# Mamba and attention in one kernel: the sums of z*C in 64x64 tiles, begun by ScalarE with D*hs, projections in quarter blocks, and new places for the extra work

## The chip, the core and the metric

The kernel runs on one core of a Trainium2 chip. The metric is the device time of one execution in microseconds; the median of the runs stands for a kernel. The engines of the core are named as the profile names them: PE is TensorE (PEld its weight loads), DVE is VectorE, ACT is ScalarE, POOL is GpSimd, SP is SyncE, whose queue issues all transfers here.

## The reference

Eight sequences of 1024 rows and 256 columns pass through a Mamba block and a layer norm, and then through a layer of attention and experts and a second layer norm. The change touches the Mamba block alone. Cut to what matters:

```python
hs, res = split(x @ w_in.T)              # 512 channels each
hs = silu(conv4(hs))                     # depthwise, 4 taps, causal
dt, B, C = split(hs @ w_xproj.T)         # 64, 16, 16 columns
delta = softplus(dt @ w_dt.T + b_dt)
# for each channel d and state n, over the rows t:
z[t] = exp(delta[t] * A) * z[t-1] + delta[t] * hs[t] * B[t, n]
y[t] = sum_n z[t, n] * C[t, n] + D * hs[t]
y = (y * silu(res)) @ w_out.T
x = layernorm(x + y)
```

## The kernel before, in words

The Mamba phase works through the eight sequences b one after the other, each in U = 64 **units** k. The 512 channels are M = 4 blocks m of 128, the 16 states NG = 8 groups g of two, and a unit takes one half j of a block (64 channels) with one group: its tile has 128 partitions, 64 channels for the first state and the same 64 for the second, and 1024 columns, the rows of the sequence. So k // 16 is the block, k // 2 % 8 the group, k % 2 the half. For each unit:

- ScalarE writes dA = exp(A * delta) (line 710), up to four units ahead,
- TensorE writes the input term delta*hs*B into PSUM with 32 small matmuls, each on a 64x64 tile of the array (`dbx`, line 404); there are two places for it, so `dbx(k)` waits until scan k-2 has ended,
- VectorE runs the scan along the columns (line 847, called scan k below); it needs `dbx(k)` and dA of the unit,
- GpSimd multiplies z by C (line 346).

Every second unit TensorE also adds a finished group to the sums over the states, three groups late, so that the products of unit k-5 are needed at unit k (`add`, line 423). It is a matmul with a stack of two identities as the weights, 128 rows onto 64 columns: four matmuls of 512 columns, one for each half of the columns and each half j of the block. The sums stand in the two PSUM banks of `pair(Y)`. At the first group of a block `d_times_hs` starts them: two 128x128 matmuls of the diagonal of D with hs (line 411). At the last group VectorE reads them in `gate` (line 828), and the next block may start when `gate` is done (`s_yg`).

Between the units stands the **extra work**: for the sequence at hand the other blocks' delta (`dt_proj`, `softplus`), u = delta*hs (`make_u`), its transposition (`turn_u`, `take_u`) and the branch of res (`res_proj`, `res_silu`), for the sequence before it the output projection, residual and layer norm (`out_proj`, `residual`, `ln_sums`, `ln_out`), and for the next one the projection of hs, the convolution and the projection to dt, B and C (`in_proj`, `take_raw`, `conv`, `hs_silu`, `x_proj`, `take_x_dbl`, `turn_b`, `make_diag`). All of it is written out by hand as `if k == ...` in the `units` function of each engine; that list of numbers is the order. Each engine works strictly in its order, so what stands behind a waiting instruction waits as well. Banks 6 and 7 of PSUM, `pair(XP)`, take the result of every one of these projections in turn: one may begin when ScalarE or VectorE has read the one before.

All matmuls have float32 operands, and the trace shows each as two instructions. After the Mamba phase, from about 1735 us, the attention phase runs; the change leaves it as it is.

## Time and profile before

| | us |
|---|---|
| median of 3 runs | 3646.37 (3645.26 to 3652.3) |
| the profiled execution | 3649.15 |
| its span, first to last instruction | 3647.3 |
| busy TensorE, VectorE, ScalarE, GpSimd | 3445.1, 3138.9, 2503.8, 1740.2 |
| one sequence of the Mamba phase, first scan to the next first scan | 212.7 |

The span holds eight such sequences, about 50 us of preparation ahead of them and the attention phase behind them. Busy time is the time in which at least one instruction of the engine was under way; matmuls are pipelined, so the distance from one start to the next says what they cost, not their own length.

### The profile page before, as it was taken

The page shows a single profiled execution, that of the slowest core. Times are in us where ns is not written, and L with a number is a line of the kernel's source. Part 1 is how long each engine was busy: PE and PEld are TensorE (multiplying, and loading weights), DVE is VectorE, ACT ScalarE, POOL GpSimd, SP SyncE. Part 2 cuts the span into 40 slices and gives each one's busy share as a digit, 9 for nine tenths or more (in the row PEclk, how much of TensorE's full clock was granted, in tenths as well). Part 3 has the DMA queues.
Part 4 walks back from the last instruction along what each step waited for, and adds up shares of the span by engine and source line. Part 5 has one row for each costly group of instructions (what it writes and reads, how often), then busy time and mean ns, then how long its engine had stood idle before and what let it go on. Part 6 is the DMA issues. An engine that isn't in the chain of part 4 may idle for free.

```text
span 3647.3 us, 119651 instructions
## 1 busy us (share of the span) xinstructions
PE 3445.1 (94%) x52062; PEld 1570.1 (43%) x52062; DVE 3138.9 (86%) x3007; ACT 2503.8 (69%) x3816; POOL 1740.2 (48%) x1562
## 2 busy tenths in 40 slices
PE   7999999999999999999599999999999999999997
PEld 4555555555555555465233323333233332332422
DVE  6898888889888888987698897998979979799796
ACT  4665656666565656664379596895967949779598
POOL 5787878878787887877121311213112121131210
PEclk9999999999999999999799999999999999999999
DMA  4444444444454544443620704207043060340700
GB/s 128 134 121 112 142 112 134 133 134 121 109 146 108 153 117 135 124 117 91 129 36 9 109 2 71 47 2 111 8 64 54 2 105 14 46 72 2 105 2 13
DMA packets 145230, 307.74 MB, mean 84 GB/s; under 512 B 24484, under 2 KB 64068, under 8 KB 144452
## 3 DMA queue, kind: packets, MB, share of 16 engines
q1 hardware_dynamic: 144708, 300.10, 35.7%
q8 instruction: 411, 6.73, 0.8%
q14 instruction: 111, 0.91, 0.1%
HBM read 230.68 MB, written 35.13 MB: 73 GB/s over the span
## 4 chain that ended last, share of the span: by engine, by line
PE 18%; ACT 12%; issue 11%; DVE 10%; DMA 0%; SPq 0%; ACTq 0%; DVEq 0%; POOL 0%
ACT probs L1509 12%; PE ps L1296 6%; PE ps L1281 4%; DVE neg_max L1623 3%; PE ps L1331 2%; PE ps L1398 2%; PE ps L1311 1%; PE ps L1343 1%; DVE acc L1775 1%; PE ps L1242 1%; DVE att L1682 1%; DVE acc L1763 1%; DVE acc L1708 1%; DVE x1T L1605 1%; DVE x1T L1603 1%
## 5 line engine op out<-in xcount | busy, mean ns | idle before, releaser
L346 POOL TENSOR_TENSOR z<-z,c_rep 128x1024 f32<-128x1024 f32 x512 | 1368.7, 2684 | 319.5 <-DVE z L847 311.6
L847 DVE TENSOR_TENSOR_SCAN z<-dA,ps 128x1024 f32<-128x1024 f32 x512 | 1158.1, 2278 | 195.5 <-PE ps L404 144.7
L1509 ACT ACTIVATE probs<-ps,e_scale 128x512 f32<-128x512 f32 x2048 | 1241.2, 702 | 116.2 <-PE ps L1281 113.9
L1623 DVE TENSOR_REDUCE neg_max<-ps 128x1 f32<-128x1024 f32 x1024 | 1187.3, 1215 | 44.3 <-PE ps L1242 43.0
L710 ACT ACTIVATE dA<-rep,a_rep 128x1024 f32<-128x1024 f32 x512 | 565.1, 1142 | 243.7 <-DVE z L847 230.8
L404 PEld LDWEIGHTS ps<-diag,u_t 64*64 64x64 f32 x32768 | 531.0, 135 | 387.0 <-issue 386.5
L1281 PE MATMUL ps<-q_st,k_st 50*128 50x512 f16 x2048 | 632.9, 384 | 31.7 <-ACT probs L1509 28.5
L404 PE MATMUL ps<-diag,u_t 64*64 64x64 f32 x32768 | 598.4, 222 | 59.4 <-DVE z L847 43.3
L1296 PE MATMUL ps<-probs,v_h 128*32 128x256 f32 x8192 | 649.4, 391 | 0.6 <-ACT o_sb L1516 0.6
L1242 PE MATMUL ps<-k_st,q_st 48*128 48x512 f16 x2048 | 600.4, 384 | 7.7 <-DVE neg_max L1623 6.8
L423 PE MATMUL ps<-z,eye 128*64 128x512 f32 x2048 | 497.1, 605 | 0.1
L1210 POOL TENSOR_TENSOR x_in<-x_in,sq_e 128x256 f32<-128x256 f32 x256 | 193.1, 754 | 407.0 <-ACT sq_e L1530 393.5
L1398 PE MATMUL ps<-w_e,x1T 128*128 128x512 f16 x1536 | 358.7, 386 | 17.3 <-DVE acc L1775 14.8
L1281 PEld LDWEIGHTS ps<-q_st,k_st 50*128 50x128 f16 x2048 | 161.1, 93 | 468.6 <-ACT probs L1509 196.7
L1193 POOL TENSOR_SCALAR m_rest<-neg_max 128x8 f32<-128x8 f32 x128 | 31.0, 242 | 669.0 <-DVE neg_max L1623 669.0
L1296 PEld LDWEIGHTS ps<-probs,v_h 128*32 128x32 f32 x8192 | 167.6, 108 | 318.4 <-issue 218.0
L1220 POOL COPY v_h<-v_all 128x80 f32<-128x80 f32 (+1 forms) x256 | 60.0, 236 | 437.6 <-PE ps L1296 437.5
L1530 ACT ACTIVATE sq_e<-ps,comb_s 128x256 f32<-128x256 f32 x256 | 106.4, 471 | 224.8 <-PE ps L1398 169.2
L1398 PEld LDWEIGHTS ps<-w_e,x1T 128*128 128x128 f16 x1536 | 145.1, 99 | 211.6 <-DVE acc L1775 28.7
L423 PEld LDWEIGHTS ps<-z,eye 128*64 128x64 f32 x2048 | 124.6, 136 | 218.5 <-issue 176.5
L1242 PEld LDWEIGHTS ps<-k_st,q_st 48*128 48x128 f16 x2048 | 152.2, 93 | 46.7 <-issue 24.3
L360 PE MATMUL ps<-xT,w_res 128*128 128x512 f32 x256 | 127.0, 618 | 0.0
(183 smaller groups left out, 2875.2 us busy)
## 6 DMA issues: line engine op xcount, KB each, us to landing
c_rep<-c_scratch SPq DMA_DIRECT2D x512, 256.0 KB, 3.9
rep<-delta SPq DMA_DIRECT2D x128, 256.0 KB, 5.5
q_st<-qk_halves SPq DMA_DIRECT2D x192, 128.0 KB, 10.0
k_st<-qk_halves SPq DMA_DIRECT2D x192, 128.0 KB, 10.7
qk_halves<-qk_parts SPq DMA_DIRECT2D x32, 512.0 KB, 10.8
x_nat<-in_x SPq DMA_DIRECT2D x9, 1024.0 KB, 7.2
x_rows<-x_nat SPq DMA_DIRECT2D x9, 1024.0 KB, 7.4
xT<-in_xT SPq DMA_DIRECT2D x8, 1024.0 KB, 7.0
```

What stands on the lines that cost most here:

```text
L346: pool.tensor_tensor(z[:, k % ZR, :], z[:, k % ZR, :], c_rep[:, slot, :], ALU.mult).then_inc(s_zc, 1)
L404: mm = pe.matmul(ps[q * QD:(q + 1) * QD, 2 + 2 * (k % 2) + r, i * TB:(i + 1) * TB], u_t[rows, i, m * P + j * QD:m * P + (j + 1) * QD], dia ...
L423: mm = pe.matmul(ps[j * QD:(j + 1) * QD, half, :], eye[:, :], z[:, (grp * QN + j) % ZR, half * HALF:(half + 1) * HALF], start=False, stop= ...
L710: act.activation(dA[:, k % AR, :], rep[:, slot, :], ACT.Exp, scale=a_rep[:, m, j, g:g + 1]).then_inc(s_da, 1)
L847: dve.tensor_tensor_scan(z[:, k % ZR, :], dA[:, k % AR, :], pair(1 + k % 2), 0.0, ALU.mult, ALU.add).then_inc(s_z, 1)
L1210: pool.tensor_tensor(to, to, scaled[:, i % 2, e, :], ALU.add).then_inc(s_pa, 1)
L1242: mm = pe.matmul(ps[:, 2 * (qt % 2) + half, :], head(q_st, half, QR, h, qt * P, P), head(k_st, half, QR, h, half * HALF, HALF), start=True ...
L1281: pe.matmul(ps[:, ring_bank(("probs", h, 2 * kt + half)), :], head(k_st, half, QM, h, kt * P, P), head(q_st, half, QM, h, half * HALF, HAL ...
L1296: mm = pe.matmul(ps[VC * j:VC * (j + 1), 6, 0:n], v_h[:, kt, :], probs[:, kt, j * n:(j + 1) * n], start=(kt == 0), stop=(kt == TT - 1), sk ...
L1398: mm = pe.matmul(ps[:, EBANK[u], :], x1T[:, x, k, t * P:(t + 1) * P], w_e[:, w, k, e2 * 2 * H:(e2 + 1) * 2 * H], start=(i == 0), stop=(i = ...
L1509: act.activation(probs[:, kt, half * HALF:(half + 1) * HALF], ps[:, ring_bank(("probs", h, 2 * kt + half)), :], ACT.Exp, scale=e_scale[:, ...
L1623: dve.tensor_reduce(neg_max[:, h % 2, qt:qt + 1], pair(qt % 2), AX.X, ALU.max, negate=True).then_inc(s_mx, 1)
```

## The change

Four things change, in the Mamba phase alone.

**The sums of z*C** are made of 64x64 tiles. `add_part` replaces `add` in the units: each group is now eight matmuls of 64 rows onto 64 columns, in two parts of four. In part 0 the first 64 rows (the first state) go to bank 0 and the last 64 to bank 1, in part 1 the other way round, so that no two row halves write to one bank at a time. Part 1 waits for the end of part 0 (`s_half`) and stands behind `dbx(k)`; part 0 of the next group waits for the end of part 1 (`s_y`).

**The start of the sums** moves from TensorE to ScalarE. `seed_sums` writes D*hs into the two banks with one activation after `gate`, and TensorE waits for it (`s_seed`) ahead of the first group of a block. Only the very first block of the run keeps its two matmuls. GpSimd builds one diagonal of D in place of four.

**Projections** are issued in quarter blocks: one matmul of 512 columns for one half of the columns and one half of the 256 contracted rows (`in_part`, `res_part`, `hs_part`), half a row block of the output projection (`out_part`), one half of `x_proj` (`x_half`) and of `dt_proj`.

**The places** of nearly all extra work change on TensorE, ScalarE and VectorE. Transfers and GpSimd's order stay.

```diff
-            def d_times_hs(m):
-                for half in range(2):
-                    pe.matmul(ps[:, half, :], d_diag[:, m, :], hs[:, m, half * HALF:(half + 1) * HALF],
-                              start=True, stop=False, skip_group_check=True)
+            def start_sums(b, m):
+                if b == 0 and m == 0:
...
+                else:
+                    pe.wait_ge(s_seed, b * M + m)
...
+            def add_part(b, grp, part):
+
+                m, g = grp // NG, grp % NG
+                if part == 0:
+                    if g == 0:
+                        start_sums(b, m)
+                    pe.wait_ge(s_zc, b * U + (grp * QN + QN + CZ))
+                    if g:
+                        pe.wait_ge(s_y, b * GR + grp + ZR // QN)
+                else:
+                    pe.wait_ge(s_half, b * GR + grp + 1)
+                for q in range(QS):
+                    rows, half = slice(q * QD, (q + 1) * QD), (q + part) % 2
+                    for j in range(QN):
+                        mm = pe.matmul(ps[j * QD:(j + 1) * QD, half, :], eye[rows, :],
+                                       z[rows, (grp * QN + j) % ZR, half * HALF:(half + 1) * HALF],
+                                       start=False, stop=(g == NG - 1), skip_group_check=True)
+                mm.then_inc(s_y if part else s_half, 1)
...
+                    if k % QN == 0 and late >= 0 and not first:
+                        add_part(late // GR, late % GR, 0)
                     dbx(b, k)
+                    if k % QN == 0 and first:
+                        add_part(late // GR, late % GR, 0)
+                    if late >= 0 and k % QN == (1 if first else 0):
+                        add_part(late // GR, late % GR, 1)
...
+            def seed_sums(b, m):
+
+                act.wait_ge(s_yg, b * M + (m + 1))
+                act.activation(pair(Y), hs[:, m, :], ACT.Copy, scale=d_col[:, m:m + 1]).then_inc(s_seed, 1)
...
+                    if k == 38:
                         res_silu(b, 2)
+                    if k == 38:
                         softplus(b, 3)
+                    if k == 38:
+                        seed_sums(b, 2)
```

**TensorE, units 36 to 42 of the first sequence, before.** L404 is `dbx`, L423 `add`, L411 `d_times_hs`, L367 the projection to delta, L360 the projection of the next sequence's hs; x32 is one unit's `dbx`.

```order
L404 MATMUL ps<-diag,u_t 64x64 x32
L367 MATMUL ps<-x_dbl,w_dt 128x512 x2
L404 MATMUL ps<-diag,u_t 64x64 x64
L411 MATMUL ps<-hs,d_diag 128x512 x2
L423 MATMUL ps<-z,eye 64x512 x4
L404 MATMUL ps<-diag,u_t 64x64 x32
L423 MATMUL ps<-z,eye 64x512 x4
L404 MATMUL ps<-diag,u_t 64x64 x32
L360 MATMUL ps<-x_nat,w_io 128x512 x4
L404 MATMUL ps<-diag,u_t 64x64 x32
L423 MATMUL ps<-z,eye 64x512 x4
L404 MATMUL ps<-diag,u_t 64x64 x32
```

The same place after the change. L405 is `dbx`, L447 `add_part` (x4 is one part), L372 the projection to delta, L360 as before.

```order
L405 MATMUL ps<-diag,u_t 64x64 x32
L447 MATMUL ps<-z,eye 64x512 x4
L372 MATMUL ps<-x_dbl,w_dt 128x512 x2
L405 MATMUL ps<-diag,u_t 64x64 x64
L447 MATMUL ps<-z,eye 64x512 x4
L405 MATMUL ps<-diag,u_t 64x64 x32
L447 MATMUL ps<-z,eye 64x512 x4
L360 MATMUL ps<-x_nat,w_io 128x512 x4
L447 MATMUL ps<-z,eye 64x512 x4
L405 MATMUL ps<-diag,u_t 64x64 x32
L447 MATMUL ps<-z,eye 64x512 x4
L405 MATMUL ps<-diag,u_t 64x64 x32
```

The two matmuls of L411 are gone, the sum of each group stands in two pieces around a `dbx`, and the four blocks of L360 stand one `dbx` earlier, at unit 39 in place of 40.

**ScalarE, units 36 to 42 of the first sequence, before.** L642 is `res_silu`, L622 `softplus`, L710 dA, L660 `take_raw`; a table load stands ahead of each change of function.

```order
L642 ACT_TABLE_LOAD
L642 ACTIVATE s_res<-ps 128x1024
L710 ACT_TABLE_LOAD
L710 ACTIVATE dA<-rep,a_rep 128x1024
L622 ACT_TABLE_LOAD
L622 ACTIVATE delta<-ps 128x1024
L710 ACT_TABLE_LOAD
L710 ACTIVATE dA<-rep,a_rep 128x1024 x5
L660 ACTIVATE sp_e<-ps 128x1024
```

The same place after, from unit 38. L757 is `res_silu`, L732 `softplus`, L753 `seed_sums`, L825 dA, L775 and L776 `take_raw`.

```order
L757 ACT_TABLE_LOAD
L757 ACTIVATE s_res<-ps 128x1024
L732 ACT_TABLE_LOAD
L732 ACTIVATE delta<-ps 128x1024
L753 ACTIVATE ps<-hs,d_col 128x1024
L825 ACT_TABLE_LOAD
L825 ACTIVATE dA<-rep,a_rep 128x1024 x3
L775 ACTIVATE sp_e<-ps 128x1024
L776 ACTIVATE hs<-ps,w_conv 128x1024
```

`res_silu`, `softplus` and the new `seed_sums` now stand in one row with no dA between them.

**VectorE, units 42 to 50 of the first sequence, before.** L847 is the scan, L796 a step of the convolution, L828 `gate`.

```order
L796 SCALAR_TENSOR_TENSOR hs<-sp_e,w_conv,hs 128x1023
L847 SCALAR_TENSOR_TENSOR z<-dA,ps 128x1024 x3
L796 SCALAR_TENSOR_TENSOR hs<-sp_e,w_conv,hs 128x1022
L847 SCALAR_TENSOR_TENSOR z<-dA,ps 128x1024
L796 SCALAR_TENSOR_TENSOR hs<-sp_e,w_conv,hs 128x1021
L847 SCALAR_TENSOR_TENSOR z<-dA,ps 128x1024
L796 SCALAR_TENSOR_TENSOR hs<-sp_w,w_conv,hs 128x1023
L847 SCALAR_TENSOR_TENSOR z<-dA,ps 128x1024
L796 SCALAR_TENSOR_TENSOR hs<-sp_w,w_conv,hs 128x1022
L847 SCALAR_TENSOR_TENSOR z<-dA,ps 128x1024
L796 SCALAR_TENSOR_TENSOR hs<-sp_w,w_conv,hs 128x1021
L847 SCALAR_TENSOR_TENSOR z<-dA,ps 128x1024
```

The same place after, units 41 to 53. L976 is the scan, L925 the convolution, L957 `gate`.

```order
L925 SCALAR_TENSOR_TENSOR hs<-sp_e,w_conv,hs 128x1023
L976 SCALAR_TENSOR_TENSOR z<-dA,ps 128x1024 x4
L925 SCALAR_TENSOR_TENSOR hs<-sp_e,w_conv,hs 128x1022
L976 SCALAR_TENSOR_TENSOR z<-dA,ps 128x1024 x2
L925 SCALAR_TENSOR_TENSOR hs<-sp_e,w_conv,hs 128x1021
L925 SCALAR_TENSOR_TENSOR hs<-sp_w,w_conv,hs 128x1023
L925 SCALAR_TENSOR_TENSOR hs<-sp_w,w_conv,hs 128x1022
L925 SCALAR_TENSOR_TENSOR hs<-sp_w,w_conv,hs 128x1021
L925 SCALAR_TENSOR_TENSOR hs<-sp_e,w_conv,hs 128x1023
L976 SCALAR_TENSOR_TENSOR z<-dA,ps 128x1024 x4
L957 TENSOR_TENSOR s_res<-s_res,ps 128x1024
L976 SCALAR_TENSOR_TENSOR z<-dA,ps 128x1024 x2
```

Five steps of the convolution, which stood behind one scan each, now stand together behind scan 47.

## Rows read from the trace of the kernel before

**Rows 1.** The page: span and busy time by engine.
```profile
span 3647.3 us, 119651 instructions
...
PE 3445.1 (94%) x52062; PEld 1570.1 (43%) x52062; DVE 3138.9 (86%) x3007; ACT 2503.8 (69%) x3816; POOL 1740.2 (48%) x1562
```

**Rows 2.** Windows: one sequence, cut at the ends of scans 8, 31, 49.
```profile
core 0: us, PE busy (x) PEld busy (x) DVE busy (x) ACT busy (x) POOL busy (x), PEclk, DMA share, GB/s
685.38:709.25 23.87, 20.37 (x558) 12.14 (x556) 22.59 (x12) 11.89 (x12) 21.97 (x9) 1.00 0.33 91
709.25:785.95 76.70, 76.05 (x1632) 45.90 (x1632) 63.84 (x45) 46.53 (x52) 57.04 (x23) 1.00 0.44 119
785.95:842.74 56.79, 54.52 (x1273) 29.77 (x1267) 48.44 (x26) 33.14 (x35) 47.91 (x18) 1.00 0.50 142
842.74:898.07 55.33, 52.29 (x1158) 28.31 (x1151) 48.57 (x27) 38.09 (x36) 46.77 (x16) 1.00 0.48 137
sum 212.69, PE 203.24 PEld 116.12 DVE 183.44 ACT 129.64 POOL 173.69; mean PE 50.81 PEld 29.03 DVE 45.86 ACT 32.41 POOL 43.42
```

**Rows 3.** Groups by line in the same sequence.
```profile
L847 DVE TENSOR_TENSOR_SCAN z<-dA,ps 128x1024 f32<-128x1024 f32 x64 | 144.8, 2278 | 25.6 <-PE ps L404 18.1 <-issue 6.4 <-ACT dA L710 1.0
L404 PE MATMUL ps<-diag,u_t 64*64 64x64 f32 x4096 | 74.7, 221 | 9.4 <-DVE z L847 5.7 <-issue 3.7
...
L423 PE MATMUL ps<-z,eye 128*64 128x512 f32 x254 | 61.7, 605 | 0.0
...
L411 PE MATMUL ps<-hs,d_diag 128*128 128x512 f32 x16 | 7.9, 618 | 0.0
```

**Rows 4.** Timeline of TensorE, units 22 to 35: start, us, instruction.
```profile
755.78 1.98 PE L411 MATMUL ps<-hs,d_diag 128*128 128x512 f32 x4
757.70 1.94 PE L423 MATMUL ps<-z,eye 128*64 128x512 f32 x8
...
785.49 2.10 PE L404 MATMUL ps<-diag,u_t 64*64 64x64 f32 x128
787.52 1.94 PE L423 MATMUL ps<-z,eye 128*64 128x512 f32 x8
789.39 1.16 PE L404 MATMUL ps<-diag,u_t 64*64 64x64 f32 x64
790.48 1.98 PE L360 MATMUL ps<-xT,w_res 128*128 128x512 f32 x4
792.39 1.16 PE L404 MATMUL ps<-diag,u_t 64*64 64x64 f32 x64
```

**Rows 5.** Timeline of TensorE, units 40 and 41.
```profile
811.12 3.70 PE L360 MATMUL ps<-x_nat,w_io 128*128 128x512 f32 x8
814.75 1.16 PE L404 MATMUL ps<-diag,u_t 64*64 64x64 f32 x64
```

**Rows 6.** Timeline of VectorE: scans, and what it waits for.
```profile
727.87 0.69 DVE L814 TENSOR_TENSOR x_nat<-x_nat,ps 128x512 f32<-128x512 f32 x1 [2.06 <-PE ps L435]
...
743.29 2.29 DVE L847 TENSOR_TENSOR_SCAN z<-dA,ps 128x1024 f32<-128x1024 f32 x1
...
786.78 6.64 DVE L847 TENSOR_TENSOR_SCAN z<-dA,ps 128x1024 f32<-128x1024 f32 x3 [0.73 <-PE ps L404]
...
815.98 2.29 DVE L847 TENSOR_TENSOR_SCAN z<-dA,ps 128x1024 f32<-128x1024 f32 x1 [2.08 <-PE ps L404]
...
879.20 2.29 DVE L847 TENSOR_TENSOR_SCAN z<-dA,ps 128x1024 f32<-128x1024 f32 x1 [2.35 <-PE ps L404]
```

**Rows 7.** Timeline of ScalarE: a scaled copy of 128x1024.
```profile
833.72 1.11 ACT L661 ACTIVATE hs<-ps,w_conv 128x1024 f32<-128x1024 f32 x1
```

**Rows 8.** Timeline of ScalarE: a table load and softplus.
```profile
672.51 1.28 ACT L622 ACT_TABLE_LOAD   x1 [2.55 <-issue]
673.80 1.02 ACT L622 ACTIVATE delta<-ps 128x1024 f32<-128x1024 f32 x1
```

More of the change, by code:

```diff
@@ L446, in last_out, with x_half @@
                     mm.then_inc(s_o, 1)
+            def x_half(c, n, m, half):
+                mm = pe.matmul(ps[0:XD, 6 + half, :], w_xp[:, m, :], hs[:, m, half * HALF:(half + 1) * HALF],
+                               start=(n == 0), stop=(n == M - 1))
+                if n == M - 1 and half == 1:
+                    mm.then_inc(s_xp, 1)
             def x_proj(c, n, m):
@@ L479, in units @@
                     late = (b * U + k) // QN - 3
[L480 to L481 removed]
+                    first = late >= 0 and late % NG == 0
+                    if k % QN == 0 and late >= 0 and not first:
+                        add_part(late // GR, late % GR, 0)
                     dbx(b, k)
[L483 to L484 removed]
@@ L528, in units @@
+                    if k == 34:
+                        res_part(b, 2, 1, 0)
+                    if k == 35:
+                        res_part(b, 2, 1, 1)
                     if k == 36:
                         pe.wait_ge(s_sr, b * M + 3)
-                        dt_proj(3)
-                    if k == 40 and more:
+                        dt_half(3, 6, 0)
+                    if k == 36:
+                        dt_half(3, 6, 1).then_inc(s_dt, 1)
+                    if k == 39 and more:
                         pe.wait_ge(s_dl, b * M + 4)
@@ new lines, in units @@
+                    if k == 52:
+                        if more:
+                            pe.wait_ge(s_he, RAW * (b * M + 4))
+                        else:
+                            pe.wait_ge(s_ut, b * M + 4)
+                        res_part(b, 3, 0, 0)
+                    if k == 52:
+                        res_part(b, 3, 0, 1)
+                    if k == 52:
+                        res_part(b, 3, 1, 0)
+                    if k == 54:
+                        res_part(b, 3, 1, 1)
@@ new lines, in units @@
+                    if k == 59 and more:
+                        pe.wait_ge(s_hs, c * M + 3)
+                        x_half(c, 2, 2, 0)
+                    if k == 59 and more:
+                        x_half(c, 2, 2, 1)
+                    if k == 59 and more:
+                        pe.wait_ge(s_hs, c * M + 4)
+                        x_half(c, 3, 3, 0)
+                    if k == 59 and more:
+                        x_half(c, 3, 3, 1)
+                    if k == 59 and more:
+                        pe.wait_ge(s_xd, c + 1)
+                        turn_b(7)
@@ L564, in units @@
+                    if k == 59 and more:
+                        dt_half(0, 6, 0)
+                    if k == 59 and more:
+                        pe.wait_ge(s_bc, c + 1)
+                        dt_half(0, 6, 1).then_inc(s_dt, 1)
+                    if k == 60 and more:
+                        turn_u(c, 0, XP)
                     if k == 56 and not more:
```

326 lines of the change are left out of this document (193 added, 133 removed).

## The prediction

> **What bounds the kernel now.** I read the page first: TensorE is busy for 94% of the span and VectorE for 86% [rows 1]. Both are means over two phases, and the change touches the Mamba phase alone, so the second view is the windows of one sequence in the middle of it, 212.69 us long [rows 2]. There TensorE is busy 203.24 us and idle 9.45, VectorE busy 183.44 and idle 29.25; ScalarE with 129.64 and GpSimd with 173.69 have more room. The granted clock is 1.00 in every window, the upper of TensorE's two levels (2.4 GHz). The groups by line say who waits: a scan stood idle for 18.1 of 25.6 us behind `dbx`, while TensorE waited 5.7 us for scans [rows 3]. So TensorE sets the pace in most of a sequence; only in the first of the four windows, the scans 0 to 8, has it 3.5 us of air in 23.87, and VectorE is the fuller one [rows 2].
>
> **Prices on TensorE**, from one start to the next. Two `dbx` in a row take 787.52 - 785.49 = 2.03 us, one ahead of a full matmul 1.09 [rows 4]: 0.94 of its own, and 0.15 for the change of the tile's shape. One `add` takes 789.39 - 787.52 = 1.87 [rows 4]. Eight instructions of full matmuls of 512 columns take 814.75 - 811.12 = 3.63 [rows 5] and four take 792.39 - 790.48 = 1.91 [rows 4], so 0.43 each, 0.86 for one matmul (a **block** below), and 0.19 for the change of shape. `add` has eight instructions of 512 columns: at 0.43 they would take 3.44 one by one, and 1.87 is two side by side (1.72) and 0.15 for the change. `dbx` has 64 instructions of 64 columns, an eighth of 0.43 each, 3.44 one by one: 0.94 is 3.7 side by side. That is the only row with four 64x64 tiles at once.
>
> **The start of the sums.** `d_times_hs` takes 757.70 - 755.78 = 1.92 [rows 4], of which 0.19 are a change of shape; without it 1.73, four times a sequence: 6.9 us less. In its place ScalarE gets an activation that no row shows, one that writes to PSUM. A scaled copy of the same size takes 1.11 [rows 7]; taken as that, it costs 4.4 us of ScalarE's 83 free ones, and nothing by itself. But TensorE waits for it, and dA is queued behind it. Bounds: 1.02 (an activation of this size [rows 8]) and twice 1.11; the difference shows only where TensorE is waiting, at most four times 1.1 us.
>
> **The sums.** A group had eight instructions two abreast, and has sixteen four abreast. At 0.43 a part is 0.86, at the packing of `dbx` 0.94. I take 0.86, since a long matmul has less start to hide. The matmuls' own time stays at 1.72 per group (bounds: 1.72 and 1.88 for four abreast; two abreast is a rival below). What goes are changes of shape: in the two orders I count 124 per sequence before and 57 after, since `add_part` has the shape of `dbx`. 67 times 0.15 to 0.19 is 10 to 12.7; I take 10.7. The waits: part 1 stands behind a `dbx` of 0.94 that covers the end of part 0. Only at the first group of a block do two parts stand together and one waits for the other's end; a matmul lasts 0.6 [rows 3] where the next starts after 0.43, so some 0.3 us, four times a sequence.
>
> TensorE's work per sequence: 203.2 - 6.9 - 10.7 = 185.6, and VectorE's stays at 183.4. Now both have the same load, and the places decide.
>
> **The places.** `dbx(k)` waits for scan k-2, so TensorE can be ahead by one scan, 2.19 us (three in 6.64 [rows 6]), and a larger heap of extra work between two `dbx` makes VectorE wait. I go through the new order by the four windows of [rows 2], with the prices above, 0.3 from the end of a `dbx` that is waited for to its scan, and 0.15 back.
>
> - Scans 0 to 8: TensorE needs 20.2 and VectorE 22.0, with two of its waits at 0.3: 22.6, from 23.9.
> - Scans 9 to 31: the output projection starts one unit earlier, but two blocks' worth of `res_part` more now stand ahead of `dbx(18)`. Summing TensorE's order from `dbx(9)`, it ends at 34.7, so scan 18 starts at 35.0, when it did before (743.29 [rows 6] - 709.25 [rows 2]). `residual(b, 1)` still waits for the fourth row block, as it did for 2.06 us [rows 6], but TensorE sets the pace there anyway. From scan 18 VectorE has 11.1 us to scan 20 and 25.2 to scan 31, and TensorE only 0.9 more: 72.2, from 76.7. Nearly all the gain of this window is in its last third.
> - Scans 32 to 49: here the new order puts more in. Blocks at units 33 to 36 cost VectorE 3 us. At unit 38 ScalarE has `res_silu`, `softplus` and the seed in a row; `softplus` starts when the projection of unit 36 ends and takes 1.28 + 1.02 [rows 8], the seed 1.11 more: TensorE waits 1.6 us for it, with `dbx(39)` behind. Then four blocks at unit 39 keep `dbx(40)` away: 3.5 us (before, 2.08 [rows 6]). Behind scan 47 the fifth convolution step needs `take_raw`, which needs four blocks of unit 49: 3.2. With 49.9 of work and 0.6 of small waits: 60.3, from 56.8. This window gets slower.
> - Scans 50 to 63: VectorE has 45.3; 0.9 for late `dbx`, and the chain from the last convolution over `x_proj`, `take_x_dbl`, `turn_b` to `make_diag` leaves it idle for 3.6 (before 2.35 for one wait of it [rows 6]): 49.8, from 55.3.
>
> The sum is 22.6 + 72.2 + 60.3 + 49.8 = 204.9, and 212.7 - 204.9 = 7.8 us per sequence. Seven sequences give 55; the last has no work for a next one and I put it at 6; the end and the start (three small products fewer on GpSimd, which something else covers) at nothing. 61 of 3649 us in the profiled execution; that one stands 2.8 above the median, so 3646.4 - 61 = 3585, and I say 3584.
>
> **The rivals.**
>
> *TensorE stays the only bound, and its idle time stays at 9.5 us*: 185.6 + 9.5 = 195.1 per sequence, 17.6 less; seven of these and 8 for the last make 131, so 3515. For it: today's order has TensorE that full. Against: VectorE has 183.4 of 195.1 to do, and its heaps (five convolution steps behind one scan) do not lie where TensorE has air. 14%.
>
> *The new places eat the gain*: my third window is worse by 3.5, and another such wait in two windows, 4 us each (the seed behind two table loads at unit 38 is the likeliest place, also for the others), brings 212.7 again: 3646, with 3630 to 3665 around it. For it: everything in the windows is near its limit. Against: TensorE has 17.6 us less to do. 11%.
>
> *Slower: the large tiles overlap less than those of `dbx`.* With two abreast a part costs 1.72, TensorE has 64 * 0.86 = 55 us more, 185.6 + 55 + 9.5 = 250 per sequence, 37 more: 3940. With three abreast a part costs 16 * 0.43 / 3 / 2 = 1.15, TensorE has 18.5 more, 185.6 + 18.5 + 9.5 = 213.6 per sequence: 3653. The gain is gone where a part is over about 1.06, if I take TensorE to set the pace in six tenths of the sequence (7.8 / 0.6 / 64 = 0.2 above 0.86). Against: `dbx` overlaps both row and column halves, with the same kinds of operands. 9%, 4 of it for two abreast. The Trainium skill, "TensorE: Matmul & The Clock Gate", Part 3 (measured speedup against the span model), speaks for it: four row tiles at once gained it a factor of 3.07 and not 4, by which a part would be an estimated 1.12; the 3.7 of `dbx` does not agree.
>
> **How the numbers follow.** The forecast itself has 66%, with 3550 to 3620: an error of 4 us per sequence either way. Two in ten may be left out: the range takes in half of the first rival and the lower part of the second, 3530 to 3632. A difference of 0.2%, 7 us, is about what can be told from none. Faster: 66, 14 and 5 of the second rival's 11 are 85%; same: 4 of the second and 3 of the third, 7%; slower: 8%.
>
> **What would show it.** Step by step in the new profile: `add_part` with four abreast, a part to the next `dbx` in 0.86 to 0.94; TensorE's busy time at 185 to 190 per sequence; the activation into PSUM at 1.0 to 1.2; VectorE idle for about 21 us, of it some 3.5 each ahead of scan 40, the fifth convolution step, and `make_diag`; windows of 22.6, 72.2, 60.3, 49.8. I am wrong if a part is over 1.0, if the third window is not slower than before, or if the sequence is under 200.

## The result, and the profile after

The changed kernel took 3721.5 us (median of four runs), the kernel before 3645.8 beside it: a ratio of 1.020, 95% interval 1.0186 to 1.0215. It is 2% slower, where I had forecast 1.7% faster and a range up to 3632.

The page of the changed kernel, its span, busy times, DMA queues and costliest groups, to be set beside [rows 1] and [rows 3]:

```profile
span 3728.7 us, 123709 instructions
...
PE 3396.3 (91%) x53962; PEld 1566.1 (42%) x53962; DVE 3156.9 (85%) x3007; ACT 2515.2 (67%) x3825; POOL 1676.7 (45%) x1559
...
q8 instruction: 427, 7.00, 0.8%
...
L976 DVE TENSOR_TENSOR_SCAN z<-dA,ps 128x1024 f32<-128x1024 f32 x512 | 1149.3, 2274 | 193.5 <-PE ps L405 134.6
...
L405 PE MATMUL ps<-diag,u_t 64*64 64x64 f32 x32768 | 622.6, 222 | 135.2 <-issue 90.0
```

The same row on the page of the kernel before:

```profile
L404 PE MATMUL ps<-diag,u_t 64*64 64x64 f32 x32768 | 598.4, 222 | 59.4 <-DVE z L847 43.3
```

TensorE is busy for 49 us less than before, and yet the span is 81 longer: both TensorE and VectorE now stand idle more. The last row is the new thing. The matmuls of `dbx` (L405) have 135.2 us of idle time ahead of them, 90.0 of it ended by "issue": nothing that the profile shows was being waited for. Before it was 59.4 us, and 43.3 of that a wait for a scan.

One sequence in the middle, in windows cut at the ends of scans 8, 31 and 49 as in [rows 2]; columns: length, then busy time of each engine, clock, DMA:

```profile
core 0: us, PE busy (x) PEld busy (x) DVE busy (x) ACT busy (x) POOL busy (x), PEclk, DMA share, GB/s
716.94:742.42 25.48, 21.22 (x652) 14.01 (x652) 22.41 (x13) 14.48 (x13) 21.98 (x9) 0.93 0.29 86
742.42:818.42 76.00, 71.64 (x1755) 44.78 (x1753) 63.12 (x45) 45.73 (x49) 56.74 (x23) 1.00 0.46 120
818.42:880.20 61.78, 56.71 (x1274) 31.22 (x1276) 53.73 (x27) 35.65 (x37) 46.15 (x19) 0.97 0.47 130
880.20:935.67 55.47, 48.25 (x1171) 25.89 (x1164) 46.14 (x26) 35.50 (x33) 40.04 (x16) 1.00 0.49 136
sum 218.73, PE 197.82 PEld 115.90 DVE 185.41 ACT 131.38 POOL 164.91; mean PE 49.46 PEld 28.97 DVE 46.35 ACT 32.84 POOL 41.23
```

The forecast was 22.6, 72.2, 60.3 and 49.8. Worked out in the same way for the second to the seventh sequence, the mean windows are 24.1, 78.5, 63.6 and 55.3 us, and 24.6, 77.0, 55.2 and 54.3 in the kernel before. So the third window became longer, as forecast, but by 8.4 us and not by 3.5. Each of the others should have become shorter by 1.3 to 5.5 us, and of them only the first did, by half a microsecond. TensorE is busy for 197.8 us, where 185.6 were forecast.

TensorE in that sequence (start, length, instructions, idle time ahead):

```profile
727.37 1.15 PE L405 MATMUL ps<-diag,u_t 64*64 64x64 f32 x58
731.19 1.29 PE L405 MATMUL ps<-diag,u_t 64*64 64x64 f32 x64 [2.67 <-DVE z L976]
732.19 2.00 PE L447 MATMUL ps<-z,eye 64*64 64x512 f32 x8
...
818.54 0.70 PE L405 MATMUL ps<-diag,u_t 64*64 64x64 f32 x33
820.28 0.69 PE L405 MATMUL ps<-diag,u_t 64*64 64x64 f32 x31 [1.03 <-issue]
...
860.22 1.09 PE L447 MATMUL ps<-z,eye 64*64 64x512 f32 x8
861.13 1.11 PE L405 MATMUL ps<-diag,u_t 64*64 64x64 f32 x64
862.06 1.04 PE L447 MATMUL ps<-z,eye 64*64 64x512 f32 x8
862.92 1.11 PE L405 MATMUL ps<-diag,u_t 64*64 64x64 f32 x64
...
910.47 5.39 PE L473 MATMUL ps<-hs,w_xp 128*96 128x512 f32 x12
916.97 1.11 PE L388 MATMUL ps<-ident,x_dbl 16*64 16x16 f32 x32 [1.11 <-ACT x_dbl L748]
```

Four things are to be seen.

- A part of the sums (L447) takes 0.91 or 0.86 us from its start to the next: the four tiles do work side by side.
- At 818.54 a `dbx` stops after 33 of its 64 instructions and goes on 1.03 us later, with no semaphore waited for.
- After 2.67 us of idle time the granted clock fell to the lower level (1.2 GHz): the part at 732.19 took 2.00 us where others take 1.04 to 1.09. The clock of the first window is 0.93.
- Six half-products of `x_proj` stand in one heap at unit 59 (5.39 us), and `turn_b` only behind them.

VectorE over the heaps at units 47 and 59, and ScalarE's seed:

```profile
866.75 1.44 DVE L925 SCALAR_TENSOR_TENSOR hs<-sp_e,w_conv,hs 128x1021 f32<-128x1021 f32 x1
868.11 6.02 DVE L925 SCALAR_TENSOR_TENSOR hs<-sp_w,w_conv,hs 128x1023 f32<-128x1023 f32 x3
874.56 1.28 DVE L925 SCALAR_TENSOR_TENSOR hs<-sp_e,w_conv,hs 128x1023 f32<-128x1023 f32 x1 [0.43 <-ACT hs L776]
875.76 4.46 DVE L976 TENSOR_TENSOR_SCAN z<-dA,ps 128x1024 f32<-128x1024 f32 x2
882.05 2.29 DVE L976 TENSOR_TENSOR_SCAN z<-dA,ps 128x1024 f32<-128x1024 f32 x1 [1.83 <-issue]
...
918.43 4.49 DVE L964 TENSOR_TENSOR diag<-eye,b_t 128x2048 f32<-128x2048 f32 x2 [4.57 <-ACT b_t L743]
```

```profile
787.82 1.10 ACT L753 ACTIVATE ps<-hs,d_col 128x1024 f32<-128x1024 f32 x1
```

Three convolution steps in a row take 6.02 us. Taken apart, the first takes 3.38 and the other two 1.28 each. In each of the seven sequences that prepare a next one the first began about 1.05 us after an instruction of GpSimd's (z times C) and ended 1.08 us behind the end of it; during the other two GpSimd stood idle. It is not the overlap alone: in the kernel before, steps behind a scan, covered by GpSimd's work for their whole length, took 1.25. `make_diag` waits 4.57 us for what `x_proj` leads to. The seed costs 1.10, as priced.

### The profile page after: what moved, and what is told of

It is laid out like the page before. It is cut to its first block, busy times and chain, and to the rows that moved or that the text cites. A ratio compares the mean times of both kernels' runs of the same rounds, so it can differ in the third digit from the quotient of the medians.

```text
span 3728.7 us, 123709 instructions
## 1 busy us (share of the span) xinstructions
PE 3396.3 (91%) x53962; PEld 1566.1 (42%) x53962; DVE 3156.9 (85%) x3007; ACT 2515.2 (67%) x3825; POOL 1676.7 (45%) x1559
## 4 chain that ended last, share of the span: by engine, by line
PE 18%; ACT 12%; issue 10%; DVE 10%; DMA 0%; SPq 0%; ACTq 0%; DVEq 0%; POOL 0%
ACT probs L1653 12%; PE ps L1440 6%; PE ps L1425 4%; DVE neg_max L1767 3%; PE ps L1475 2%; PE ps L1542 2%; PE ps L1455 1%; PE ps L1487 1%; PE ps L1386 1%; DVE acc L1919 1%; DVE att L1826 1%; DVE acc L1907 1%; DVE acc L1852 1%; DVE x1T L1749 1%; DVE x1T L1747 1%
## 5 line engine op out<-in xcount | busy, mean ns | idle before, releaser
L347 POOL TENSOR_TENSOR z<-z,c_rep 128x1024 f32<-128x1024 f32 x512 | 1306.6, 2569 | 459.5 <-DVE z L976 453.6
L976 DVE TENSOR_TENSOR_SCAN z<-dA,ps 128x1024 f32<-128x1024 f32 x512 | 1149.3, 2274 | 193.5 <-PE ps L405 134.6
L825 ACT ACTIVATE dA<-rep,a_rep 128x1024 f32<-128x1024 f32 x512 | 570.8, 1144 | 337.4 <-DVE z L976 329.4
L405 PEld LDWEIGHTS ps<-diag,u_t 64*64 64x64 f32 x32768 | 589.0, 136 | 433.7 <-issue 431.1
L405 PE MATMUL ps<-diag,u_t 64*64 64x64 f32 x32768 | 622.6, 222 | 135.2 <-issue 90.0
L447 PE MATMUL ps<-z,eye 64*64 64x512 f32 x4048 | 570.6, 612 | 12.2 <-issue 7.4
L447 PEld LDWEIGHTS ps<-z,eye 64*64 64x64 f32 x4048 | 122.8, 136 | 111.7 <-issue 84.4
L360 PE MATMUL ps<-x_nat,w_io 128*128 128x512 f32 x224 | 115.5, 657 | 16.1 <-ACT hs L776 14.8
```

What stands on the lines that cost most here:

```text
L347: pool.tensor_tensor(z[:, k % ZR, :], z[:, k % ZR, :], c_rep[:, slot, :], ALU.mult).then_inc(s_zc, 1)
L405: mm = pe.matmul(ps[q * QD:(q + 1) * QD, 2 + 2 * (k % 2) + r, i * TB:(i + 1) * TB], u_t[rows, i, m * P + j * QD:m * P + (j + 1) * QD], dia ...
L447: mm = pe.matmul(ps[j * QD:(j + 1) * QD, half, :], eye[rows, :], z[rows, (grp * QN + j) % ZR, half * HALF:(half + 1) * HALF], start=False, ...
L825: act.activation(dA[:, k % AR, :], rep[:, slot, :], ACT.Exp, scale=a_rep[:, m, j, g:g + 1]).then_inc(s_da, 1)
L976: dve.tensor_tensor_scan(z[:, k % ZR, :], dA[:, k % AR, :], pair(1 + k % 2), 0.0, ALU.mult, ALU.add).then_inc(s_z, 1)
```

## Where TensorE's instructions come from

The page has a DMA queue of kind "instruction", q8. It brought 427 packets of 16,384 bytes each (7.00 MB). The trace has 53,962 matmuls of TensorE, as many weight loads and 1,521 instructions of its sequencer, 109,445 in all: 427 times 256 and 133 more. So a packet holds 256 instructions of 64 bytes, and this queue is TensorE's. From the trace of the changed kernel, 250 to 1680 us, I took the start and end of every such packet, and every idle time of over 0.2 us ahead of a matmul of `dbx` that the profile ends with "issue".

- Of 52 such gaps 49 end 1.2 to 1.6 us behind the end of a packet. By chance it would be 4 (a band of 0.4 us, times 245 packets in 1430 us, is 7%). In the kernel before it is 15 of 16: the same thing, seldom.
- Counting TensorE's instructions from the start of the program settles it. Each of the 52 gaps stands ahead of an instruction with the same remainder on division by 256, 193, so exactly at the edge of a packet; so do all 16 of the kernel before, and all 539 in the fifteen kernels here with the full stream and no added increments. Of the 44 idle times of this length ahead of `dbx` that a semaphore ended, none does. These gaps are instructions that had not arrived.
- No packet starts while more than 298 of the instructions that have come are still to run (301 in any kernel here, in the same stretch). It takes 1.16 us (the median), and its first instruction runs 1.2 to 1.6 us later, 2.4 to 2.8 us from its start. A `dbx` with its weight loads is 128 instructions, so 298 of them are at most 2.2 us of `dbx` after `dbx` at 0.94. By this estimate any longer run of `dbx` outlasts its supply.
- Two packets never start closer than 3.4 us. That is not what held TensorE up in these gaps: the packets that ended them started 3.9 to 12.7 us behind the one before, 6.0 in the median. They came late for the pace at which `dbx` used up what was there.

That became theory S (supply). The rival, theory P (places): the heaps and long chains of the new order make the scans wait, whatever the stream.

This table is worked out from the traces: mean per sequence over the second to the seventh, between the starts of the scans named in the head, and time at the lower clock level. The last column is a row of the profile: idle time ahead of `dbx` that "issue" ended, all of 250 to 1680 us together, which is 6.3 to 7.2 sequences.

```
                sequence  0-9  9-20  20-32 32-40 40-50 50-57 57-64 | low clock | issue, total
before           211.1   25.4  42.3  34.6  23.3  32.4  27.1  26.1 |  1.1      |  14.0
seed_old         205.8   24.9  42.4  32.9  24.0  30.7  24.9  26.1 |  1.7      |  18.7
tiles_old        210.0   27.2  41.2  33.1  23.6  33.0  25.7  26.3 |  2.9      |  19.2
both_old         209.8   27.4  41.6  32.1  24.7  32.4  25.2  26.4 |  6.3      |  30.7
joined           213.6   25.0  43.8  33.6  24.4  33.6  26.7  26.5 |  3.4      |  53.2
places_only      228.6   25.8  45.1  34.9  28.8  37.8  26.0  30.2 | 12.0      |  40.3
after            221.5   24.8  44.6  33.3  28.1  36.7  23.6  30.5 | 10.2      |  67.9
few_before       205.2   24.6  41.4  33.8  21.7  32.1  25.9  25.9 |  0.6      |   0.3
few_seed_old     199.6   23.9  41.6  31.9  21.8  30.4  23.9  26.2 |  1.1      |   0.3
few_both_old     201.1   27.2  40.5  30.4  22.2  30.6  24.3  25.9 |  5.7      |   0
few_after        208.2   22.7  43.3  28.4  25.0  35.6  23.6  29.6 | 12.0      |   1.4
seed_units0      204.3   23.8  42.0  33.1  23.7  30.6  25.1  26.1 |  2.3      |  13.1
tiles_units0     207.8   24.1  42.5  32.5  24.6  32.8  25.1  26.2 |  2.8      |  42.5
```

## The experiments

Where kernels are set against each other below, the differences are those of their ratios, on 3650 us. The intervals of the ratios make such a difference uncertain by some 6 us for the closest and 12 for the widest.

### One part of the change at a time

**tiles_old** is the kernel before with `add_part`:

```
-                    if k % QN == 0 and late >= 0 and late % NG:
-                        add(late // GR, late % GR)
+                    if k % QN == 0 and late >= 0 and not first:
+                        add_part(late // GR, late % GR, 0)
                     dbx(b, k)
...
+                    if late >= 0 and k % QN == (1 if first else 0):
+                        add_part(late // GR, late % GR, 1)
```

> The kernel before with one part of the change: the sums of z*C in 64x64 tiles (add_part), begun by the two full matmuls of d_times_hs as before, everything in its old place. Theory P (the new places do the harm: heaps of extra work at units 17, 39, 49, 52 and 59 that the scans must wait out): the tiles take changes of shape away and cost nothing, so faster than before, 3590 to 3625 us. Theory S (supply: the instruction packets of TensorE, 256 instructions each, never start closer than 3.4 us, and in the changed kernel most gaps inside dbx end 1.35 to 1.5 us behind the end of such a packet; the tiles add 48 instructions and their weight loads per group of four units): the 96 more per group eat what the shape changes give, 3640 to 3690 us, with the idle time of dbx put down to 'issue' at twice that of before or more.

Measured: 3655.5 us, ratio 1.0022 (1.0012 to 1.0032). The count in this expectation is wrong: a group is two units, and the tiles add 8 matmuls and 8 weight loads to it. The time is in theory S's range, and theory P alone falls. But the "issue" time of `dbx` did not double (19.2 us for 14.0), so more late instructions are not what cost the gain here. The table has it in the first window, 27.2 us for 25.4; that is taken up below.

**seed_old** is the kernel before with `start_sums` and `seed_sums`:

```
-                    d_times_hs(m)
+                    start_sums(b, m)
...
+                act.activation(pair(Y), hs[:, m, :], ACT.Copy, scale=d_col[:, m:m + 1]).then_inc(s_seed, 1)
```

> The kernel before with one other part: ScalarE begins the sums with D*hs (at units 4, 22, 37 and 52), the sums themselves as before, everything else in its old place. Both theories: TensorE has 6.9 us per sequence less to do and slightly fewer instructions, faster, 3600 to 3635 us. A third theory, Q (the seed is late in ScalarE's queue and the first sum of a block waits for it): 3646 or more, with idle time of TensorE behind the seed of 1 us or more at each block.

Measured: 3611.7 us, ratio 0.9899 (0.9884 to 0.9914). TensorE's busy time fell from 204.4 to 197.5 us per sequence, by the 6.9 forecast, and the sequence by 5.3. This part is a plain gain, 37 us; theory Q falls.

**both_old** has both, with every piece of extra work in its old place.

> The kernel before with tiles and seed, all extra work in its old places: the change without its new places and quarter blocks. Theory P: 3560 to 3600 us, as the prediction had it or better. Theory S: 3640 to 3680, since the instruction stream is as thick as in the changed kernel. If it lands between 3600 and 3640, both have a share.

Measured: 3636.1 us, ratio 0.9964 (0.9952 to 0.9975): beside the seed, the tiles cost 24 us.

**places_only** is the changed kernel with `add` and `d_times_hs` as before and without the seeds.

> The changed kernel with the sums as before (add in 64x128 tiles, d_times_hs on TensorE): only the new places and quarter blocks. Theory P: slower than the changed kernel, 3730 to 3800, since TensorE has 17 us per sequence more to do in the same places. Theory S: between the two kernels, 3660 to 3720, with fewer 'issue' gaps in dbx than the changed kernel's 74 us.

Measured: 3772.8 us, ratio 1.033 (1.0309 to 1.035), as theory P had it. From both_old to the changed kernel the places cost 86 us. They are the largest cause, and their loss lies in the windows of scans 9 to 20, 32 to 50 and 57 to 64.

### The instruction stream thinned

In four kernels `dbx` is issued as 8 matmuls of 256 columns in place of 32 of 64, on the same tiles and with the same sum of columns, so that a `dbx` is 32 instructions with its weight loads and not 128; the operands of three of four blocks of time are left out:

```
-                for i in range(NI):
+                for i in range(0, NI, 4):
...
-                                           diag[rows, i, g * QS + q, :], start=True, stop=True)
+                                           diag[rows, i:i + 4, g * QS + q, :], start=True, stop=True)
```

**few_before**

> The kernel before, with TensorE's instruction stream thinned: dbx is issued as 8 matmuls of 256 columns instead of 32 of 64, on the same four 64x64 tiles and with the same number of columns in all. It leaves out three quarters of the products' operands (four blocks of time share the u_t of the first of them), so its values are not the reference's; the work of every other engine is the same. 128 instructions of TensorE with their weight loads become 32 per dbx. Theory S (supply): the gaps inside dbx with 'issue' as their end, 12 to 14 us in six sequences, vanish, 3610 to 3640. Without it: 3646 or a little more, if long columns overlap less.

Measured: 3605.4 us, ratio 0.9864 (0.9847 to 0.988), 50 us less and just under both ranges. It is not all supply, because the thinned `dbx` is also cheaper on the array:

```profile
709.90 1.09 PE L404 MATMUL ps<-diag,u_t 64*64 64x256 f32 x16
710.92 3.72 PE L435 MATMUL ps<-w_io,s_res 128*128 128x256 f32 x16
```

Ahead of a full matmul it takes 710.92 - 709.90 = 1.02 us, where the full one took 1.09 [rows 4]. In both kernels nearly every undisturbed one takes just that, 1.092 and 1.024. Times 64 it is 4.4 us of the 5.9 that the sequence fell by, an estimated 35 of the 50. Some 15 are left for the supply, about the "issue" time that went (14.0 us to 0.3, in nearly seven of eight sequences).

**few_both_old**

> The kernel with tiles and seed in the old places, its dbx thinned in the same way (the same work left out). It measured 3636 with the full stream. Theory S: now the tiles bring what the prediction counted on, 3550 to 3590. If the tiles' gain is lost elsewhere (the end of a group's sums comes two units later in ScalarE's and VectorE's queues, since part 1 stands behind a dbx): 3615 to 3640.

Measured: 3567.9 us, ratio 0.9765 (0.975 to 0.9779).

**few_after**

> The changed kernel, its dbx thinned in the same way (the same work left out). It measured 3721. Theory S: the stream was what turned its heaps into waits, so it falls to 3600 to 3640 and comes within 40 us of the thinned kernel in the old places. Theory P (heaps of extra work and long chains make the scans wait, whatever the stream): it stays 70 to 90 us behind the thinned kernel in the old places, 3640 to 3690.

Measured: 3616.2 us, ratio 0.9893 (0.9877 to 0.9909). Thinning took 112 us off the changed kernel and 73 off the one in the old places; some 35 of each is again the cheaper `dbx`. The groups by line of this kernel, 250 to 1680 us; in the same stretch of the changed kernel `dbx` had 104.9 us of idle time ahead, 67.9 of it "issue":

```profile
L976 DVE TENSOR_TENSOR_SCAN z<-dA,ps 128x1024 f32<-128x1024 f32 x451 | 1006.3, 2271 | 90.5 <-PE ps L405 50.7 <-issue 37.3 <-PE ps L447 1.9
...
L405 PE MATMUL ps<-diag,u_t 64*64 64x256 f32 x7212 | 491.8, 388 | 65.4 <-DVE z L976 63.6 <-issue 1.4
```

The "issue" gaps are gone, and what is left is a wait for scans. The other half stands as well: thinned, the new places still cost 47 us (86 with the full stream). Both theories have a share. The difference of 39 is about that of the "issue" times, 67.9 and 30.7 us in the stretch; that the array time saved makes some waits shorter as well is not excluded. And the pair few_before and few_after tells what the whole change costs where instructions are not late: 11 us (give or take 9), in place of 73.

**few_seed_old** thins the kernel with the seed alone.

> The kernel with the seed alone in the old places (3612 us), its dbx thinned to 8 matmuls of 256 columns (the same work left out as in the other thinned kernels). Set against the thinned kernel with tiles and seed, 3568 us. If supply alone kept the tiles from paying: the tiles must pay here, so this one is slower than that, 3590 to 3610. If TensorE's time was not what bounded the windows that the tiles shorten: 3560 to 3575, no difference.

Measured: 3561.0 us, ratio 0.9758 (0.9739 to 0.9777), no slower than few_both_old, as its second outcome had it. So the tiles bring nothing even without a supply limit. The table says where it goes: they shorten scans 9 to 32 by 2.6 us per sequence, and lose 3.3 in scans 0 to 9.

**stream_only** is seed_old with empty instructions, as many as the tiles bring:

```
+                for _ in range(16):
+                    pe.sem_inc(s_extra, 1)
                 mm.then_inc(s_y, 1)
```

> The kernel with the seed alone in the old places (3612 us), with 16 more instructions on TensorE per group of two units, as many as the tiles bring: increments of a semaphore that nobody waits for, behind each sum, no work on the array. Theory S: two more instruction packets per sequence and more 'issue' gaps inside dbx (19 us in six sequences before), 3620 to 3645. If the thicker stream is no cost: within 5 us of 3612.

Measured: 3726.7 us, ratio 1.0221 (1.0194 to 1.0248), far past both. It is not the clean test that I meant. Its timeline of TensorE shows that the 16 increments take 0.4 us themselves ahead of each `dbx`, 32 times a sequence, 13 of the 14.7 us:

```profile
803.85 1.94 PE L429 MATMUL ps<-z,eye 128*64 128x512 f32 x8
806.22 1.16 PE L406 MATMUL ps<-diag,u_t 64*64 64x64 f32 x64 [0.44 <-issue]
```

### Why the first window is late with the tiles

**joined** is both_old with parts 0 and 1 next to each other ahead of `dbx`:

```
                     if k % QN == 0 and late >= 0 and not first:
                         add_part(late // GR, late % GR, 0)
+                        add_part(late // GR, late % GR, 1)
                     dbx(b, k)
```

> Tiles and seed in the old places (3636 us), but both parts of a group's sums stand together ahead of dbx, with no dbx between them. If the lateness of part 1 is what costs the tiles their gain (the window of scans 0 to 8 took 27.4 us there and 24.9 with the seed alone, since the gate behind scan 3 waits for the last group's part 1, which is behind dbx(4)): 3600 to 3625, and that window near 25 us. If not: part 1 now waits some 0.3 us for part 0's end at each of 32 groups, 3636 to 3700.

Measured: 3669.1 us, ratio 1.0047 (1.003 to 1.0064). The first window did come back to 25.0 us, so there the split is what makes the gate late: behind scan 3 VectorE waits for part 1 of the last group, which stands behind `dbx(4)`, and the scans behind the gate. From 250 to 1680 us the gates wait 19.1 us in both_old, 8.4 in joined and 6.2 in seed_old. But five of the six later windows became longer, and the "issue" time ahead of `dbx` went from 30.7 to 53.2 us. As a cure it fails.

### The new places, one stretch at a time

Each of these is the changed kernel with one stretch of extra work back in its old places, on TensorE, ScalarE and VectorE. The core of the first one's edit:

```
-                    if k == 49 and more:
-                        hs_part(c, 2, 0, 0)
...
+                    if k in (48, 49) and more:
+                        in_proj(w_hs, x_next, 2, 6, k - 48, s_ih)
...
-                    if k == 47 and more:
-                        conv(c, 1, 1)
...
+                    if k in (47, 48, 49) and more:
+                        conv(c, 1, k - 46)
```

**units44_old**

> The changed kernel (3721 us), with the extra work of units 44 to 54 back in its old places on TensorE, ScalarE and VectorE: the blocks of w_io spread over units 44 to 51 instead of eight at unit 49, the convolution steps one per unit instead of five at unit 47. Theory P: the window of scans 40 to 49, 36.7 us against 32.4 in the old places, gives 4 us back in each of seven sequences: 3685 to 3700. If the heap was no cost and only the thick stream was: 3710 to 3725.

Measured: 3703.1 us, ratio 1.0144 (1.0114 to 1.0174): 20 us of the 86, and 3 us above theory P's range. Here the convolution step of 3.4 us is gone in six of seven sequences, 2.1 us each, which is part of it. The window of scans 40 to 49 fell from 36.7 to 31.5, as forecast, and the next one took 3.4 of it back (scans 50 to 56: 27.0, from 23.6).

**units55_old**

> The changed kernel, with the extra work of units 55 to 63 back in its old places: x_proj at units 55, 56 and 58, turn_b at 59, dt_half at 60, turn_u at 63, and what ScalarE and VectorE do with them. Theory P: the window of scans 57 to 63, 30.4 us against 26.4, gives 4 us back in each of seven sequences: 3685 to 3700. Otherwise 3710 to 3725.

Measured: 3693.8 us, ratio 1.0118 (1.009 to 1.0145): 30 us, as forecast. Its timelines of VectorE and TensorE, where the changed kernel had `make_diag` behind 4.57 us of waiting:

```profile
899.19 2.29 DVE L971 TENSOR_TENSOR_SCAN z<-dA,ps 128x1024 f32<-128x1024 f32 x1 [2.13 <-PE ps L405]
901.39 2.27 DVE L959 TENSOR_TENSOR diag<-eye,b_t 128x2048 f32<-128x2048 f32 x1
903.58 2.28 DVE L971 TENSOR_TENSOR_SCAN z<-dA,ps 128x1024 f32<-128x1024 f32 x1
```

```profile
894.36 3.67 PE L473 MATMUL ps<-hs,w_xp 128*96 128x512 f32 x8
897.96 1.16 PE L405 MATMUL ps<-diag,u_t 64*64 64x64 f32 x64
899.38 1.11 PE L388 MATMUL ps<-ident,x_dbl 16*64 16x16 f32 x32 [0.26 <-ACT x_dbl L744]
```

With a `dbx` ahead of `turn_b` a scan can run while ScalarE takes `x_dbl`, and `make_diag` then finds `b_t` ready.

**units9_old**

> The changed kernel (3721 us), with the extra work of units 9 to 20 in its old places (out_proj whole at units 10 to 16, the residuals behind scans 13 to 16). The window of scans 9 to 19 took 44.6 us against 41.6 in the old places, with the residual of the second row pair waiting 4.3 us for out_part. If this stretch is a culprit by itself: 3695 to 3705. If it pays back later: 3710 to 3725.

Measured: 3702.9 us, ratio 1.015 (1.0121 to 1.018): 18 us, as the first outcome had it; its window fell from 44.6 to 42.3. In the changed kernel VectorE reaches the second residual early and waits 4.33 us for `out_part` (2.06 before [rows 6]).

**units33_old**

> The changed kernel (3721 us), with the extra work of units 33 to 43 in its old places: res(2) at units 30 and 34, dt at 36, the four blocks of w_io at 40, and on ScalarE res_silu at 36, softplus and the seed at 37. The window of scans 32 to 39 took 28.1 us against 24.7 in the old places. If this stretch is one of the culprits by itself: 3 to 3.5 us of each of seven sequences, 3695 to 3705. If it pays back later: 3710 to 3725.

Measured: 3738.4 us, ratio 1.0248 (1.0227 to 1.0269): slower, which neither outcome allowed. Scans 32 to 49 together took 64.3 us against 64.8, no change; my border at scan 40 had cut through the heap that merely moved from unit 39 to 40. And scans 20 to 31 took 2.2 longer. Here `res_proj` stands at unit 30 and waits for `take_u`, which in this mixture comes at ScalarE's unit 31, behind the new place of `turn_u`. The stretch can't be judged by this kernel.

### Better versions

**best_tiles** and **best_seed** take the new places of units 0 to 8 and 21 to 31 alone, with and without tiles.

> Tiles and seed in the old places (3636 us), but the extra work of units 0 to 8 and 21 to 31 in the new ones, since these two windows (scans 0 to 8 and 20 to 31) were shorter in the thinned changed kernel than in the thinned one in the old places, by 4.5 and 2.0 us. If windows add up: 7 times 4 to 6.5 less, 3590 to 3610. If what one window gains the next one pays back (TensorE's stream and the scans are chained over the border): 3625 to 3640.

> The same places, with the seed by ScalarE but the sums in 64x128 tiles as before: against the seed alone in the old places, 3612 us. If the places of units 0 to 8 and 21 to 31 are good by themselves: 3585 to 3605. Against the kernel with tiles in these places it tells once more what the tiles are worth with the full stream: theory S says that this one is faster by 10 to 30 us.

Measured: 3655.9 us, ratio 1.0016 (1.0001 to 1.0032), and 3641.9 us, ratio 0.9974 (0.9964 to 0.9985); with all places old it was 3636 and 3612. The labels promise what the runs don't keep. The first window gained what was forecast (23.7 for 24.9 with the seed alone), but scans 40 to 49, whose places had not changed, took 34.5 in place of 30.7. Windows don't add up.

**tiles_units0** and **seed_units0** take those of units 0 to 8 alone:

```
-                    if k == 2:
-                        dt_proj(1)
-                    if k == 8:
+                    if k == 0:
+                        dt_half(1, 6, 0)
+                    if k == 0:
+                        dt_half(1, 6, 1).then_inc(s_dt, 1)
+                    if k == 6:
                         turn_u(b, 1, XP)
```

> Tiles and seed, with the extra work of units 0 to 8 in the new places (dt_half at unit 0, turn_u at 6, make_u behind scan 4) and everything else in the old ones. In the old places it took 3636 us, its first window 27.4 us; that window takes 24.2 to 24.8 us wherever these places are new. If the window's gain stays: 3610 to 3620. If it is paid back later in the sequence, as in units33_old and best_tiles: 3630 to 3645.

> The same places with the seed alone and the sums in 64x128 tiles: 3612 us in the old places, its first window 24.9 us, with the new places of units 0 to 8 it was 23.7 us. 3600 to 3610 if the 1.2 us stay. Set against the kernel with tiles in the same places: if the tiles pay once their late first window is mended, this one is slower than that; if the supply of instructions takes their gain, it is faster by 5 to 20 us.

Measured: 3618.4 us, ratio 0.9913 (0.9899 to 0.9927), and 3601.8 us, ratio 0.9857 (0.984 to 0.9874). Both are faster than the kernel before, and the seed with the new places of units 0 to 8 is the fastest version of this study, 1.4% under it. Between these two the first window and the clock are alike (24.1 and 23.8 us; 2.8 and 2.3 us at the lower level), and the idle time ahead of `dbx` that "issue" ended is not: 42.5 us against 13.1. Those 29 us fall in seven of the eight sequences, and the tiles cost 20 (ratios 0.9913 and 0.9857). All of these gaps stand at the edge of a packet, so the supply can take the tiles' gain here and more; that it alone does so is concluded from the sizes.

## Why the prediction was wrong, step by step

**The prices held.** A part takes 0.86 to 0.91 us (0.86 taken), the seed 1.10 (1.11), and `d_times_hs` gave back 6.9 us of TensorE's time per sequence (6.9). The rival with tiles that overlap less falls: it decided at 1.06. The figure of the Trainium skill, "TensorE: Matmul & The Clock Gate", Part 3 (a factor of 3.07 for four row tiles), by which a part would have been an estimated 1.12, doesn't agree with this row-and-column tiling.

**The step that failed: the arrival of TensorE's instructions was put at nothing.** The prediction summed TensorE's order by its array time, 0.94 for a `dbx`, and let it catch up behind each heap at that pace. A heap of long matmuls is few instructions, but the catching up behind it is 128 per `dbx`, and at 0.94 that is faster than they came: 52 gaps of `dbx`, each at the edge of a packet, and 67.9 us of "issue" time where it had been 14.0. With the stream thinned the change costs 11 us in place of 73. So of the 134 us between the forecast (61 faster) and the result (73 slower), some 62 go with the supply. The new places lose 86 us with the full stream and 47 with the thinned one.

**The second step: the waits that the new places bring were priced too low.** The thinned pair leaves 72 of the 134 us to this, to the term below and to the clock. The windows of [rows 2] were forecast at 72.2, 60.3 and 49.8 from the second on, and are 78.5, 63.6 and 55.3. The heaps at units 39 and 47 were seen, but the row of convolution steps at unit 47 was priced at its bare length, and takes 2.1 us more. The chain at unit 59 was put at 3.6 us of idle time; it is 4.57 for `make_diag` alone, since six half-products of `x_proj` stand in a row ahead of `turn_b` with no `dbx` between them. The residual was called harmless; undoing that stretch gave 18 us. One reading was off too: it took its 35.0 for the start of scan 18 to be that of the kernel before, which is 743.29 - 709.25 = 34.0.

**"67 times" a change of shape, 10.7 us, was mis-sized.** The count was right: in the traces a sequence has 125 changes before and 59 after (124 and 57 in the prediction). But a change is worth less than 0.15 to 0.19. Tiles_old has 51 fewer than the kernel before, and TensorE's busy time fell by 5.1 us per sequence. Both_old has 55 fewer than seed_old; of the thinned pair with the same two orders (191.8 and 187.9) busy time fell by 3.9, and by 6.2 if half of the 4.6 us more at the lower clock is put aside. That is 0.07 to 0.11 each, so an estimated 5 to 7 us in place of 10.7.

**The clock, which the prediction left at 1.00.** It falls more often in the changed kernel: 10.2 us per sequence at the lower level against 1.1. At 16 of its 17 falls in six sequences the engine had just stood idle for 1.6 to 4.0 us, as in the rows at 731.19. Not every such wait brings a fall: of 33 idle times of over 1.5 us in these sequences 16 did; the kernel before had nine of them and two falls. At half speed that is up to 5 us of the array's time per sequence. No run separates its cost from that of the waits which bring it about. In both_old it is 6.3 against 1.7 in seed_old, which may be some 16 of the tiles' 24 us there; that is argued, not shown. The thinned pair, too, has 12.0 against 0.6 us, so the clock may be a good part of the 72 us above.

**What closes and what doesn't.** In time on 3650 us: the seed -37, the tiles beside it +24, the places beside both +86, in all +73. Of the 86, units 9 to 20, 44 to 54 and 55 to 63 give 18, 20 and 30 when undone alone, each give or take 12. The remaining 18 stay open: the stretches interact, and units 33 to 43 could not be judged. The rival "the new places eat the gain" was right in kind, but its 3646, and 3665 at most, were too low as well: it priced two more waits and left the supply at nothing too.

## What to carry to other kernels

Count instructions as well as columns: where an engine runs hundreds of small matmuls, look for gaps ended by "issue" within one line, and whether they stand at every 256th instruction, before trusting array time as the pace at which it can catch up. Splitting matmuls into smaller tiles buys array time with instructions; here it never paid. Where a stream is thinned as a test, measure first what the thinned instructions cost by themselves; here that was 35 us of an effect of 50. A heap of extra work between dependent steps costs its own length, the catching up behind it, and possibly the clock; and since a stretch hands its lateness on, judge places by the whole sequence and not by a window.

## What the runs showed of the hardware

- TensorE's instructions came in packets of 256 (16 KB, 1.1 to 1.2 us each) during the run. All 539 "issue" gaps of over 0.2 us inside `dbx`, in fifteen kernels between 250 and 1680 us, stood exactly at the edge of a packet, and no packet started there with more than 301 instructions still to run. In a kernel whose TensorE looked 94% busy this cost an estimated 15 us of 3650, and in the changed one some 62 more.
- The same columns on the same four 64x64 tiles took 0.07 us less as 8 matmuls of 256 columns (1.02 us ahead of a full matmul) than as 32 of 64 (1.09).
- 16 increments of a semaphore in a row on TensorE cost 0.4 us ahead of the next matmul.
- A convolution step on VectorE that followed another one and began 1.05 us into a multiply of GpSimd's took 3.38 us and ended 1.08 us behind it; with GpSimd idle it took 1.28. Steps behind a scan, under the same multiply, took 1.25 in the kernel before and at most 1.7 in the changed one. Why the two differ is open.
